# The end stage of a Mamba and mixture-of-experts layer: biases as three bf16 rows, one of two gain multiplications on GpSimd, and a store moved behind the last tile loads

## The reference, cut to what matters

```python
x = L0_attn_x
xn = _layernorm(x, axis=-1)
x = x + _L0_attn_ref(xn, ...) + _L0_ffn_ref(xn, ...)

# end of _L0_attn_ref (Mamba)
out = y @ W_out + b_out
res = out + x                      # x is xn here
mu = jnp.mean(res, axis=-1, keepdims=True)
var = jnp.var(res, axis=-1, keepdims=True)
return (res - mu) * jax.lax.rsqrt(var + LN_EPS) * ln_g + ln_b

# end of _L0_ffn_ref (experts); xf is xn, row by row
y = jnp.einsum('teh,ehd->ted', h, w2) + b2
out = jnp.einsum('ted,te->td', y, combine)   # weighted sum of the token's two experts
out = _ln(out + xf, ln_g, ln_b)    # the same normalisation with a gain and bias of its own
```

## Time and profile before

| | us |
|---|---|
| median of 3 runs | 1838.35 (1836.94 to 1839.93) |
| the profiled execution | 1839.68 |
| its span in the profile | 1837.7 |
| TensorE busy | 1580.6 (86%) |
| VectorE busy | 1545.9 (84%) |
| ScalarE busy | 1458.0 (79%) |
| GpSimd busy | 968.3 (53%) |

### The profile page before, as it was taken

The page is one execution under the profiler, slowest core; times in us unless marked ns, Lnnn a source line. Parts: engine busy times, 40 slices in busy tenths (PEclk is TensorE's granted clock), DMA queues, the critical chain, the costliest instruction groups (busy, mean ns, idle before and its releaser), DMA issues.

```text
span 1837.7 us, 28368 instructions
## 1 busy us (share of the span) xinstructions
PE 1580.6 (86%) x6978; PEld 967.1 (53%) x6978; DVE 1545.9 (84%) x2529; ACT 1458.0 (79%) x2552; POOL 968.3 (53%) x563
## 2 busy tenths in 40 slices
PE   5988389898889888998989898889898998975899
PEld 4555145555556555555555555555555655542344
DVE  4767489999999998989998989999998989811997
ACT  3545379898988989898988889898989898944676
POOL 2767756565555556556655565565556555612000
PEclk9777789999999999999999999999999999988899
DMA  7999743433433333334343333333333333323984
GB/s 236 346 290 350 256 112 83 106 97 83 110 82 93 96 93 85 105 85 107 83 108 91 87 97 91 98 83 100 89 94 85 105 85 108 82 39 75 276 270 148
DMA packets 182857, 234.69 MB, mean 128 GB/s; under 512 B 45865, under 2 KB 148524, under 8 KB 182719
## 3 DMA queue, kind: packets, MB, share of 16 engines
q1 hardware_dynamic: 141234, 171.83, 30.3%
q0 software_dynamic: 26160, 36.06, 10.5%
q10 hardware_dynamic: 15328, 25.20, 4.1%
HBM read 149.33 MB, written 83.70 MB: 127 GB/s over the span
## 4 chain that ended last, share of the span: by engine, by line
DVE 33%; ACT 25%; PE 21%; issue 13%; DMA 4%; ACTq 3%; POOL 1%; SPq 0%; another core or an unknown queue 0%; DVEq 0%; POOLq 0%
DVE area L1276 7%; DVE area L1289 5%; ACT area L660 4%; DVE area L1306 4%; DVE area L1285 3%; PE psX L975 3%; ACT psD L654 3%; PE psT L1023 3%; DVE more L1338 3%; ACT h_T L694 3%; ACT L702 3%; ACT L699 3%; DMA area<-L_attn_x 2%; DVE more L1335 2%; DVE h_norm L1319 2%
## 5 line engine op out<-in xcount | busy, mean ns | idle before, releaser
L539 POOL TENSOR_TENSOR area<-area,more 128x1024 f32<-128x1024 f32 x258 | 604.4, 2360 | 553.2 <-DVE area L1289 279.2
L1306 DVE TENSOR_TENSOR area<-area,psD 128x1024 f32<-128x1024 f32 x256 | 310.1, 1211 | 0.2 <-PE psD L988 0.2
L965 PE MATMUL psH<-w_sb,ffn_xT 128*128 x544 | 265.8, 612 | 5.8 <-ACT ffn_xT L670 5.7
L975 PE MATMUL psX<-w_sb,h_T 128*128 x1088 | 267.0, 389 | 0.8 <-ACT y_out L676 0.8
L516 POOL DMA_INDIRECT expert_d<-y_out,meta x139 | 220.7, 1588 | 83.3 <-ACT y_out L676 56.9
L996 PE MATMUL psY<-ident,area 128*128 128x128 f32 x2048 | 250.7, 276 | 0.0
L975 PEld LDWEIGHTS psX<-w_sb,h_T 128*128 128x128 f32 x1088 | 205.8, 193 | 60.6 <-issue 32.4
L660 ACT ACTIVATE area<-area,A_sb 128x512 f32<-128x512 f32 x258 | 171.5, 712 | 74.2 <-DVE area L1289 40.8
L996 PEld LDWEIGHTS psY<-ident,area 128*128 128x128 f32 x2048 | 222.2, 141 | 13.4
L694 ACT ACTIVATE h_T<-psT,be_T,g_T 128x128 f32<-128x128 f32 x540 | 202.2, 459 | 4.7 <-PE psT L955 4.7
L654 ACT ACTIVATE psD<-area,A_sb 128x512 f32<-128x512 f32 x258 | 177.9, 690 | 31.6 <-DVE area L1276 12.3
(11 more groups left out here) (186 smaller groups left out, 2515.4 us busy)
## 6 DMA issues: line engine op xcount, KB each, us to landing
more<-B_rows_d SPq DMA_DIRECT2D x130, 512.0 KB, 4.0
xin<-sorted_x SPq DMA_DIRECT2D x137, 128.0 KB, 2.1
more<-ssm_d SPq DMA_DIRECT2D x18, 512.0 KB, 3.7
area<-xnT_d SPq DMA_DIRECT2D x17, 512.0 KB, 3.5
mamba_d<-mo_stage SPq DMA_DIRECT2D x17, 512.0 KB, 2.9
area<-L_attn_x SPq DMA_DIRECT2D x8, 1024.0 KB, 6.9
xnT_d<-w_sb ACTq DMA_DIRECT2D x16, 512.0 KB, 6.6
expert_d<-area ACTq DMA_DIRECT2D x8, 1024.0 KB, 8.9
```

Source lines behind the costliest of these rows:

```text
L539: pool.tensor_tensor(inflow[:, k], dtx, B_rep[par][:, k].rearrange("p (a t) -> p a t", a=1).to_broadcast([P, KD, CHUNK]), ALU.mult).then_i ...
L965: nc.tensor.matmul(psH[:, :], ffn_xT[:, k, :], w1_sb[:, bass.ds(e, 1), k, :].rearrange("p o h -> p (o h)"), start=(k == 0), stop=False)
L975: nc.tensor.matmul(psX[:, DIM:2 * DIM], h_T[:, buf, k, :], w2_sb[:, bass.ds(e, 1), k, :].rearrange("p o d -> p (o d)"), start=(k == 0), st ...
L1306: V.tensor_tensor(h, h, C_rep[k].rearrange("p (a t) -> p a t", a=1) .to_broadcast([P, KD, CHUNK]), ALU.mult).then_inc(S[f"hC{k}_done"], 1)
```

## The change

1. **Biases.** `ln_b` and `fln_b` are loaded with the other biases at the start, added on VectorE (columns 50 to 52 of `bsplit`), split into three bf16 parts with them and written to DRAM as `eb_parts_d`. In the end stage they are read back as `eb_rows`, three rows, the 256 columns twice, and one product of 512 columns replaces the two of fp32. GpSimd's add is gone, and so are two broadcasts of 128 KB.
2. **Expert half.** `er1` is multiplied by its gain on GpSimd (in a loop of its own, 128x512), `er0` on VectorE as before. TensorE waits for `e_gain` ahead of the Mamba half and for the new `e_gain1` ahead of the expert half.
3. **SyncE's order.** The loads of the last seven tiles stand ahead of the last `store_mamba`.

```diff
-        e_g0, e_g1, e_b0, e_b1 = (more_again.take(DIM) for _ in range(4))
+        e_g0, e_g1 = (more_again.take(DIM) for _ in range(2))
+        eb_rows = more_again.take(DIM).bitcast(BF16)[0:PARTS, :]
...
         end_loads = [(dst, everywhere(v)) for dst, v in
-                     ((e_g0, ln_g), (e_g1, fln_g), (e_b0, ln_b), (e_b1, fln_b))]
+                     ((e_g0, ln_g), (e_g1, fln_g))]
+        end_loads += [(eb_rows[:, t * DIM:(t + 1) * DIM], eb_parts_d) for t in range(2)]
...
-                             (bsplit[:, 48:50], b_out)):
+                             (bsplit[:, 48:50], b_out), (bsplit[:, 50:52], ln_b), (bsplit[:, 52:54], fln_b)):
...
-            sp.wait_ge(S["b_split_out"], 48)
+            sp.dma_start(eb_parts_d.rearrange("r (p c) -> p r c", p=P), bsplit_bf[:, :, 50:52]).then_inc(S["b_split_out"], 16)
+            sp.wait_ge(S["b_split_out"], 64)
...
-            store_mamba(CHUNKS)
             for u in range(MAMBA_TURNS, FFN_TURNS):
                 load_tile(u + 2, (u + 2) % RING)
+            store_mamba(CHUNKS)
...
             pool.wait_ge(S["w_end"], 16 * len(end_loads))
-            pool.tensor_tensor(e_b0, e_b0, e_b1, ALU.add).then_inc(S["e_bias"], 1)
-            pool.wait_ge(S["e_bias"], 1)
+            gain1 = e_g1.rearrange("p (o d) -> p o d", o=1).to_broadcast([P, 2, DIM])
+            with pool.Fori(0, TILES // 2 // END_RING) as k:
+                for q in range(END_RING):
+                    pool.wait_ge(S["e_norm"], k * END_RING + q + 1)
+                    pool.tensor_tensor(er1[q], er1[q], gain1, ALU.mult).then_inc(S["e_gain1"], 1)
...
             pe.wait_ge(S["mo_copied"], 2 * CHUNKS + 2)
-            pe.wait_ge(S["e_bias"], 1)
+            pe.wait_ge(S["w_end"], 16 * len(end_loads))
...
-                    for t in range(2):
-                        nc.tensor.matmul(total[:, t * DIM:(t + 1) * DIM], ones[0:1, :], e_b0[0:1, :], start=False, stop=False)
+                    nc.tensor.matmul(total, ones_bf[:, :], eb_rows, start=False, stop=False)
                     pe.wait_ge(S["e_gain"], k * END_RING + q + 1)
                     nc.tensor.matmul(total, ident[:, :], er0[q].rearrange("p t d -> p (t d)"), start=False, stop=False)
+                    pe.wait_ge(S["e_gain1"], k * END_RING + q + 1)
                     nc.tensor.matmul(total, ident[:, :], er1[q].rearrange("p t d -> p (t d)"), start=False, stop=True
...
-            dve.wait_ge(S["biases_in"], 48)
+            dve.wait_ge(S["biases_in"], 80)
+            V.tensor_tensor(bsplit[:, 50:52], bsplit[:, 50:52], bsplit[:, 52:54], ALU.add).then_inc(S["e_bias"], 1)
+            dve.wait_ge(S["e_bias"], 1)
...
-                for v, gain in ((er0, e_g0), (er1, e_g1)):
-                    a = V.tensor_tensor(v[q], v[q], two(gain), ALU.mult)
-                a.then_inc(S["e_gain"], 1)
+                V.tensor_tensor(er0[q], er0[q], two(e_g0), ALU.mult).then_inc(S["e_gain"], 1)
```

7 lines of the change are left out of this document (4 added, 3 removed).

## The result

The changed kernel takes 1810.59 us, the median of four executions (1809.28 to 1820.4), and the kernel before, run beside it, 1839.14 (1836.94 to 1844.03). The ratio is 0.985, with an interval of 0.981 to 0.989.

What follows compares the result with a forecast made beforehand. The prediction took TensorE and VectorE, both full, to bound the end stage. Savings of 8.7 + 1.9 + 1.8 + 0.5 + 3.7 = 16.6 us gave a forecast of 1821.7 us, range 1816.5 to about 1829.

Steps and rivals of the forecast that it cites:

- The start: Start of the kernel: two more 1 KB loads, one VectorE add and a fourth split row cost nothing, bound 1 us.
- The first loads: End stage's first loads: two small loads replace two 128 KB broadcasts, saving 0.5 us, bounds 0 and 0.75.
- The tail: Last pair, from its normalisation's end to the copy out: 3.3 us instead of 5.1, saving 1.8, bounds 1 and 2.4.
- The turns: End stage's repeated turn per pair of token tiles: P = 3.58 us after the change, 95.9 us against 104.6, saving 8.7.
- the path over the root: End-stage turn: averages, then ScalarE's Ln and Exp, then VectorE's small L1474 keep the turn at least 3.44 us.
- No collision: Rival, 22%: VectorE's and GpSimd's multiplications don't delay each other in the end stage; turn 3.44 us, total 1818.1 us.
- DMA engines as the bound: Rival, 12%: transfers stop at 280 GB/s and set the end stage's pace; turn 3.75 us, total 1826.1 us.
- all of GpSimd's time on VectorE: Rival, 4%: GpSimd's whole multiplication delays VectorE each end-stage turn; turn 4.59 us, total 1849.9 us.
- The clock in the turns: Rival, 2%: TensorE's clock stays at 1.2 GHz in the end stage; turn 5.6 us, total 1880 us or more.
- SyncE's move: Rival, 8%: moving the last store gives nothing, since something else holds tile 130 as long; total 1825.4 us.
- First four turns: End stage's first four turns: less VectorE work ahead of TensorE and shorter bias passes save 1.9 us, bounds 1 and 2.5.
- SyncE's order: Before the end stage: loads ahead of the last store remove TensorE's wait at tile 130, saving 3.7 us, bounds 2 and 4.3.

Runs made afterwards that it cites:

- double_gain1: The changed kernel with a second GpSimd multiplication, by ones, behind each of the expert half's, TensorE waiting for both: 1839.18 us.
- no_gain1: The changed kernel without the expert half's multiplication by its gain on GpSimd: 1804.84 us.
- order_only: The kernel before with only the last tiles' loads moved ahead of the last store: ratio 0.999 to the kernel before.
- bias_only: The kernel before with the new start and the biases as three bf16 rows, both multiplications on VectorE, old SyncE order: ratio 0.997 to the kernel before.
- start_again: The kernel before with only the changed start (two more 1 KB loads, VectorE's add, fourth split row), on a chip of usual speed: 1840.67 us, ratio 1.000.
- before_again: The kernel before, word for word, profiled once more: 1836.01 us.
- changed_again: The changed kernel, word for word, on another chip beside the kernel before: 1819.67 us, ratio 0.989.

## Why the prediction was right or wrong

The path that sets the turns was right. The step that failed is "*The start.* ... Nothing, bound 1 us", the only account of what lies ahead of the last scan, together with a range made from costs of the change alone: 10.3 us came from there in this comparison, and they put the time below 1816.5. The first loads were mis-sized (0.5 for 3.0), but with 3.0 the forecast would have been 1819.2, still inside the range. In the tail the size was near and the reason wrong.

**The turns (8.7 us, P = 3.58).** Measured: from the fifth normalisation (1703.13) to the last (1799.15) 96.0 us against 104.6, so 8.5. 26 intervals of 3.58 and one of 2.94. GpSimd's 1.26 by the line through two sizes was 1.27; the bias product's record 0.385 was 0.38. The step that carried it was to count where VectorE's multiplication would start against GpSimd's. double_gain1 tests it away from the value it was made for: 4.26 against 4.21. That the 3.58 came out to the hundredth is in part luck: the path over the root was 3.48 and not 3.44 (no_gain1), and the collision cost 0.10 and not 0.14. TensorE's turn, which the prediction had as 2.83 and at most 3.2, is 3.09 where it runs without waits; in the turns that costs nothing.

**The rivals.** No collision would have shown 3.44, DMA engines as the bound 3.75, all of GpSimd's time on VectorE 4.59; measured 3.58. The clock in the turns was 1.00. SyncE's move did give its part (order_only).

**First four turns (1.9).** From the first x product to the fifth normalisation 22.1 against 23.8: 1.7. This stretch isn't steady: with the old end stage it took 22.4 to 23.8 us in five traces.

**The tail (1.8).** 3.63 against 5.10: 1.5. I had counted the wait of one multiplication for the other, and two products behind it. But the tail is 3.62 with both multiplications on VectorE (bias_only) and 3.63 with none on GpSimd (no_gain1): TensorE is behind there and works without a wait, and each pair takes it 3.09 us in place of 3.83. The bias product alone gives the 1.5. That GpSimd's multiplication ends behind VectorE's, named as a sign of being wrong, did happen in the last two turns, but the last product didn't wait for it.

**SyncE's order (3.7).** 4.5. From the last scan to tile 130's transpose the traces differ by 4.4 (36.6 to 32.2 us), the 4.3 us of idle time; from there to the stage's first load they agree, 54.3 and 54.1. I had taken off 0.6 for time that would fall to the half clock, and none did: over this stretch, from the last scan to the stage's first load, TensorE was granted 0.91 before and 0.92 now. (The window from 1640 to 1680 is granted 0.88 now, but it ends in the idle time ahead of the end stage, which comes 15 us earlier.)

**The first loads (0.5).** The size that was wrong: "256 KB at the 348 GB/s of that stretch". It measured 3.0. The rate was read from a window in which the pairs' loads run, not from the broadcasts' own landings, which were in the trace. The upper bound of 0.75 was wrong with it.

**The start (0).** VectorE's first statistics did stay where they were (14.07 us, 14.05 before), and by start_again the median doesn't move. But "nothing" was wrong as an account of the 1600 us ahead of the last scan. The main loop took 1357.2 and 1366.0 us in two traces of the changed kernel, and 1357.2 to 1368.6 over all fourteen, as its clock fell or not. The first comparison had a changed kernel with a high clock in three executions of four, against a kernel before whose trace has the fallen one. 10.3 us of the 29.6 lie there: 7.5 in the loop, and 2.8 ahead of it, where before_again and changed_again swap the same values (231.1 and 234.1). Nor is it chance alone: with the changed start, 14 of 36 executions on the chips of this speed had a mean clock of 0.954 or more, and of before none of the 30 on the two later ones. How the start does that stays open. The repetition gave 1819.67 us with its kernel before at 1838.16, inside the range. The range was made only from costs of the change; it had no term for this, though three executions of before, 1836.94 to 1839.93, couldn't have shown it.

By the last three stretches alone, the forecast was 16.6 and the measurement 19.3, and the 2.7 between are the first loads (2.5) and SyncE (0.8), less some 0.7 in the other three terms.

## What to carry to other kernels

When a part of an engine's work moves to another one that it can't run beside, count where in the turn the two meet: the price is how far the first one's end overshoots the second one's start, and here an order of work took it away. When two engines are full, an edit for one of them alone can be worth little, and its value can't be added to the other's: here 2.3 and 3.3 us alone, 11.7 together. Price a transfer by its own time from issue to landing, not by the rate of a stretch beside it, and look for a part of the kernel, untouched by the change, whose time differs between executions before a whole time is compared.

## What the runs showed of the hardware

A VectorE multiplication of 128x512 with both inputs in SBUF that met GpSimd's ended 0.54 us after it, whether it came 0.08, 0.33 or 0.87 us into it; the GpSimd one that came 0.04 us behind VectorE's took 1.77 us in place of 1.27. Four broadcasts of one 1 KB row to 128 partitions landed 1.4 us apart, 93 GB/s if taken one by one, where the pairs' loads reach 348; two of them more or less moved the stage's first product by 2 to 3 us. TensorE's clock fell to the lower level for stretches of a long, evenly busy loop, not always in the same places in two executions of one kernel, and nowhere behind 250 us in some; this went with 7 to 9 us of 1360. On one chip the first stage took 66 to 88 us longer and the others about as long as elsewhere.
